# A layer's norms, recurrence and small network in one plan, its roots as GpSimd powers

## The reference, cut to what matters

```python
x = x + _mamba(_layernorm(x, ln1_g, ln1_b), in_proj_w, conv_w, ...)
h = _layernorm(x, ln2_g, ln2_b)
h = relu(einsum('btd,hd->bth', h, w1) + b1)      # 512 hidden
x = x + einsum('bth,dh->btd', h, w2) + b2
```

## Time and profile before

| | us |
|---|---|
| Median of three runs | 3910.06 (3905.43 to 3916.63) |
| The profiled execution | 3907.57, its span 3906.2 |
| Last layer, stages 1 and 2, to the first convolution | 2353.4 to 2413.1 |
| Stage 3 | 2413.1 to 2779.2 |
| Stage 4 | 2779.5 to 2875.5 |
| Stage 5 | 2876.0 to 3906.2 |

### The profile page before, as it was taken

The page is one execution under the profiler, slowest core; times in us unless marked ns, Lnnn a source line. Parts: engine busy times, 40 slices in busy tenths (PEclk is TensorE's granted clock), DMA queues, the critical chain, the costliest instruction groups (busy, mean ns, idle before and its releaser), DMA issues.

```text
span 3906.2 us, 43056 instructions
## 1 busy us (share of the span) xinstructions
PE 3027.4 (78%) x15912; PEld 1384.5 (35%) x16002; DVE 2560.6 (66%) x2915; ACT 2032.3 (52%) x3628; POOL 1557.2 (40%) x938
## 2 busy tenths in 40 slices
PE   4899989755678777777767798766778888888876
PEld 2233333412223222223224524211335555554544
DVE  4888724399987888888883243877446565565553
ACT  1566641344567676676662213676345556555544
POOL 2221101134566666766672011444234444344432
PEclk7899989766788888777878798888789998998998
DMA  3222100211111221121120002001000000000000
GB/s 87 46 43 41 26 2 0 79 38 26 36 37 32 48 45 37 37 50 40 27 47 11 1 0 77 22 22 27 6 10 20 20 11 20 10 20 20 10 16 26
DMA packets 79742, 114.48 MB, mean 29 GB/s; under 512 B 16270, under 2 KB 49422, under 8 KB 78106
## 3 DMA queue, kind: packets, MB, share of 16 engines
q1 hardware_dynamic: 68268, 103.06, 11.0%
q0 software_dynamic: 11264, 8.66, 1.6%
HBM read 37.70 MB, written 17.33 MB: 14 GB/s over the span
## 4 chain that ended last, share of the span: by engine, by line
PE 48%; DVE 22%; ACT 15%; issue 7%; POOL 3%; DMA 2%; SPq 1%; POOLq 0%; DVEq 0%; ACTq 0%
DVE layer_mamba_state L1348 8%; DVE psum L1336 4%; PE psum L1120 3%; PE psum L2468 3%; ACT layer_mamba_decay L1274 3%; PE psum L2499 3%; PE psum L1197 3%; PE psum L783 2%; PE psum L236 2%; PE psum L2162 2%; PE psum L248 2%; PE psum L242 2%; PE psum L913 2%; PE psum L2552 2%; ACT L1274 2%
## 5 line engine op out<-in xcount | busy, mean ns | idle before, releaser
L1377 POOL TENSOR_TENSOR layer_mamba_state<-layer_mamba_state,layer_mamba_c 128x1024 f32<-128x1024 f32 x320 | 781.2, 2450 | 593.2 <-DVE layer_mamba_state L1348 588.6
L1348 DVE TENSOR_TENSOR_SCAN layer_mamba_state<-layer_mamba_decay,psum 128x1024 f32<-128x1024 f32 x320 | 731.5, 2286 | 44.4 <-ACT layer_mamba_decay L1274 12.0
L1197 PE MATMUL psum<-layer_mamba_state,two_to_one 128*64 128x512 f32 x1280 | 440.1, 780 | 127.7 <-DVE layer_mamba_x L1365 82.2
L1274 ACT ACTIVATE layer_mamba_decay<-layer_mamba_delta_wide,layer_weights 128x511 f32<-128x511 f32 x640 | 415.8, 711 | 77.6 <-DMA layer_mamba_delta_wide<-layer_mamba_delta 42.3
L1336 DVE TENSOR_TENSOR psum<-psum,layer_mamba_u_wide 128x1024 f32<-128x1024 f32 x320 | 393.3, 1229 | 65.4 <-PE psum L1155 27.5
L724 DVE TENSOR_REDUCE layer_peak<-psum 128x2 f32<-128x1024 f32 x256 | 308.6, 1221 | 95.0 <-PE psum L695 90.2
L796 ACT ACTIVATE layer_exps<-psum 128x1024 f32<-128x1024 f32 x256 | 256.0, 1023 | 149.8 <-PE psum L763 149.7
L2865 POOL TENSOR_TENSOR layer_p<-layer_p,layer_stats 128x512 f32<-128x512 f32 x128 | 133.2, 1041 | 297.8 <-DVE layer_stats L2788 297.7
L2659 ACT ACTIVATE layer_p<-psum,layer_stats 128x128 f32<-128x128 f32 x512 | 181.5, 369 | 128.4 <-DVE layer_stats L2781 128.0
L2852 POOL TENSOR_TENSOR layer_qk<-layer_qk,layer_v_between 128x1024 f32<-128x1024 f32 x64 | 150.5, 2351 | 218.2 <-DVE layer_v_between L2752 216.4
L1155 PE MATMUL psum<-layer_mamba_bc,layer_mamba_pick 96*64 96x512 bf16 x768 | 165.0, 457 | 87.0 <-DVE psum L1336 63.3
(11 more groups left out here) (349 smaller groups left out, 6072.9 us busy)
## 6 DMA issues: line engine op xcount, KB each, us to landing
layer_mamba_delta_wide<-layer_mamba_delta SPq DMA_DIRECT2D x160, 128.0 KB, 2.4
layer_mamba_u_wide<-layer_mamba_work SPq DMA_DIRECT2D x160, 128.0 KB, 2.4
layer_v_between<-layer_v SPq DMA_DIRECT2D x16, 512.0 KB, 4.3
qk_dram<-layer_qk_parts SPq DMA_DIRECT2D x16, 384.0 KB, 2.9
layer_q_rows<-qk_dram SPq DMA_DIRECT2D x96, 64.0 KB
layer_k_rows<-qk_dram SPq DMA_DIRECT2D x96, 64.0 KB
layer_v_between<-layer_v SPq DMA_DIRECT2D x16, 384.0 KB, 5.6
layer_weights<-weights_dram SPq DMA_DIRECT2D x1, 4147.0 KB, 14.2
```

The lines of the kernel that those rows point to most:

```text
L1197: e = pe.matmul(c.psum[j * HALF:(j + 1) * HALF, self.sum_banks[h], :], c.two_to_one[:, :], self.state[i % len(self.state)][:, j, :], start ...
L1274: e = act.activation(decay[:, j, 1:SEQ], self.delta_wide[h][:, j, 1:SEQ], ACT.Exp, scale=rates[:, rate:rate + 1])
L1348: dve.tensor_tensor_scan(state, decay, self.fill.rearrange("p j t -> p (j t)"), 0.0, ALU.mult, ALU.add).then_inc(self.scanned, 1)
L1377: pool.tensor_tensor(state, state, self.both(self.c_wide[turn % self.C_BUFFERS][:, :]), ALU.mult).then_inc(self.multiplied, 1)
```

## The change

Stages 1 to 4 become one stage with one plan. `NormBeside` replaces `Norm` there, three times: "norm3" (x to xn, called O below), "norm1" (F) and "norm2" (S). Of each one sequence is in flight. Its root and reciprocal are one GpSimd power (add eps on ScalarE by Identity, then `pow` -0.5 on a 128x4 tile). The normed input has two buffers instead of eight, the hidden tile one instead of two. The small network's steps are planned behind S. z's silu moves next to x's. TensorE starts behind `conv_made`. The mask and tables on GpSimd are due at 50. In stage 5 the due times move: make 7.8 apart for 7.5, weigh 11.6 behind its score for 10.4, and the norm's, gates' and pass's. After the barrier each engine has one more drain.

```diff
-    start=40.0, pace=4.4, item=0.0, spread=-3.4, c_spread=-3.0, copy=-2.0, decay=-4.5, conv=((0.2, 0.8, 1.4, 2.0),), x=(2.7,), z=2.6, z_gate=3.2,
+    start=85.0, pace=4.4, item=0.0, spread=-3.4, c_spread=-3.0, copy=-2.0, decay=-4.5, conv=((0.2, 0.8, 1.4, 2.0),), x=(2.9,), z=2.6, z_gate=2.95,
...
-MAKE_PACE3, WINDOW_PACE3, TURN_AFTER3 = 7.5, 6.5, 8.0
+NORMS3 = (-10.9, -7.8, 3.6)
+STEPS3 = (0.0, 2.0, 3.2, 5.0, 6.8, 7.8, 10.0, 12.2, 13.2)
+HIDDEN_PACE3, TABLES3 = 1.2, 50.0
+MAKE_PACE3, WINDOW_PACE3, TURN_AFTER3, WEIGH_AFTER3 = 7.8, 6.5, 8.0, 11.6
 MAKE3 = [2.0 + MAKE_PACE3 * t for t in range(BLOCKS)]
 ROOT3 = MAKE3[-1] + 6.5
 SCALE3 = [ROOT3 + 2.6 + 2.1 * t for t in range(BLOCKS)]
 TURN3 = [SCALE3[0] + 2.4 + 2.5 * t for t in range(BLOCKS)]
 SCORE3 = [TURN3[1] + 3.0 + WINDOW_PACE3 * m for m in range(WINDOWS3)]
-OUT3 = SCORE3[-1] + TURN_AFTER3 + 4.6
-NORM3 = [OUT3 + 6.4 + t for t in (0.0, 1.3, 2.1, 2.8, 3.9, 5.6, 5.9, 8.0, 8.8)]
-GATE3 = NORM3[-1] + 1.0
+OUT3 = SCORE3[-1] + WEIGH_AFTER3 + 2.2
+NORM3 = [OUT3 + 6.4 + t for t in (0.0, 1.3, 2.4, 4.4, 5.4, 6.4, 7.6, 8.8, 9.8)]
+GATE3 = NORM3[-1] + 2.6
 MLP3 = GATE3 + 9.8
-PASS3 = MLP3 + 5.0
+PASS3 = MLP3 + 6.0
 UPDATE3 = PASS3 + 0.2
...
+        self.conv_made = c.sem(ctx, "conv_made")
+    def make_conv(self):
+        pool, hold, w = self.c.pool, self.c.pool_hold, self.w
         by_tap = lambda t: t.rearrange("p (k e) -> p k e", k=8)
-        hold.wait_ge(loaded, 16)
+        hold.wait_ge(self.loaded, 16)
         pool.tensor_tensor(by_tap(self.conv[""][:, :]), by_tap(w["conv_rows"]),
-                           w["w_x"].rearrange("p (o e) -> p o e", o=1).broadcast_to([P, 8, P]), ALU.mult)
+                           w["w_x"].rearrange("p (o e) -> p o e", o=1).broadcast_to([P, 8, P]), ALU.mult).then_inc(
+            self.conv_made, 1)
+    def tables(self, wf, ffn_loaded):
+        pool, hold, w = self.c.pool, self.c.pool_hold, self.w
+        yield TABLES3
         pool.tensor_copy(self.mask[:, :], w["masks"])
         hold.wait_ge(ffn_loaded, 16)
...
+class NormBeside:
+    def __init__(self, c, ctx, banks, name, src, out, times, gain=None, bias=None):
...
+        c.pool.memset(self.power[:, :], -0.5).then_inc(self.power_set, 1)
+        self.done = self.scaled if gain is None else self.biased
...
+    def pe(self, ready):
+        c, pe, hold = self.c, self.c.pe, self.c.pe_hold
+        hold.wait_ge(c.constants_made, c.constants)
+        for b in range(SEQS):
+            start = self.times(b)
+            yield start
+            at = self.banks.take((self.name, "mean", b), start, start + STEPS3[1] + 0.9)
+            if ready:
+                hold.wait_ge(ready, b + 1)
+            c.wait_bank(at)
+            pe.matmul(c.psum[:, at, :], c.mean_of[:, :], self.src(b), start=True, stop=True).then_inc(self.mean_made, 1)
+            c.bank_read[at] = self.mean_taken, b + 1
+            now = start + STEPS3[3]
+            yield now
+            at = self.banks.take((self.name, "var", b), now, start + STEPS3[4] + 0.4)
+            hold.wait_ge(self.squared, b + 1)
+            c.wait_bank(at)
+            for j in range(BLOCKS):
+                m = pe.matmul(c.psum[:, at, j:j + 1], self.square[:, j * P:(j + 1) * P], c.mean_of[:, 0:1], start=True,
+                              stop=True)
+            m.then_inc(self.var_made, 1)
+            c.bank_read[at] = self.var_kept, b + 1
+            now = start + STEPS3[6]
+            yield now
+            at = self.banks.take((self.name, "spread", b), now, start + STEPS3[7] + 0.9)
+            hold.wait_ge(self.inverse_made, b + 1)
+            c.wait_bank(at)
+            for j in range(BLOCKS):
+                m = pe.matmul(c.psum[:, at, j * P:(j + 1) * P], self.scale[:, 1, j:j + 1].broadcast_to([P, P]),
+                              c.ident[:, :], start=True, stop=True)
+            m.then_inc(self.spread_made, 1)
+            c.bank_read[at] = self.scaled, b + 1
+    def act(self, free):
+        c, act, hold = self.c, self.c.act, self.c.act_hold
+        for b in range(SEQS):
+            start = self.times(b)
+            yield start + STEPS3[2]
+            hold.wait_ge(self.mean_taken, b + 1)
+            act.activation(self.square, self.centred, ACT.Square).then_inc(self.squared, 1)
+            yield start + STEPS3[4]
+            hold.wait_ge(self.var_made, b + 1)
+            act.activation(self.scale[:, 0, :], self.bank("var", b)[:, 0:BLOCKS], ACT.Identity, bias=c.eps[:, :]).then_inc(
+                self.var_kept, 1)
+            if self.gain is not None:
+                yield start + STEPS3[8]
+                signal, value = free
+                hold.wait_ge(signal, value(b))
+                hold.wait_ge(self.scaled, b + 1)
+                act.activation(self.out(b), self.centred, ACT.Identity, bias=self.bias).then_inc(self.biased, 1)
+    def dve(self):
+        dve, hold = self.c.dve, self.c.dve_hold
+        for b in range(SEQS):
+            start = self.times(b)
+            yield start + STEPS3[1]
+            hold.wait_ge(self.mean_made, b + 1)
+            hold.wait_ge(self.done, b)
+            dve.tensor_tensor(self.centred, self.src(b), self.bank("mean", b), ALU.subtract).then_inc(self.mean_taken, 1)
+            yield start + STEPS3[7]
+            hold.wait_ge(self.spread_made, b + 1)
+            if self.gain is None:
+                dve.tensor_tensor(self.out(b), self.centred, self.bank("spread", b), ALU.mult).then_inc(self.scaled, 1)
+            else:
+                dve.scalar_tensor_tensor(self.centred, self.centred, self.gain, self.bank("spread", b), ALU.mult,
+                                         ALU.mult).then_inc(self.scaled, 1)
+    def pool(self):
+        pool, hold = self.c.pool, self.c.pool_hold
+        hold.wait_ge(self.power_set, 1)
+        for b in range(SEQS):
+            yield self.times(b) + STEPS3[5]
+            hold.wait_ge(self.var_kept, b + 1)
+            pool.tensor_tensor(self.scale[:, 1, :], self.scale[:, 0, :], self.power[:, :], ALU.pow).then_inc(
+                self.inverse_made, 1)
 class Attention3:
...
+    def __init__(self, c, ctx, x, xn, w, loaded, setup, out, tables):
+        self.c, self.x, self.xn, self.w, self.loaded, self.out = c, x, xn, w, loaded, out
+        self.normed = [c.buffer(ctx, f"normed{s}", [P, SEQ]) for s in range(2)]
+        self.inner = c.buffer(ctx, "mlp_normed", [P, SEQ])
+        self.hidden = c.buffer(ctx, "hidden", [P, HID_BLOCKS3, SEQ])
+        self.more = c.buffer(ctx, "more", [P, SEQ])
+        self.banks = Banks(5)
+        self.mamba = mamba = Mamba(c, ctx, w, loaded, setup.conv, 1, 8, SEQS, ("",), PLAN3, self.banks, 5, (7,))
+        self.opening = NormBeside(c, ctx, self.banks, "norm3", lambda b: x[:, b, :], lambda b: xn[:, b, :],
+                                  lambda b: PLAN3.front(b, NORMS3[0]))
+        self.first = NormBeside(c, ctx, self.banks, "norm1", lambda b: xn[:, b, :], lambda b: self.normed[b % 2][:, :],
+                                lambda b: PLAN3.front(b, NORMS3[1]), w["ln1_g"], w["ln1_b"])
+        self.second = NormBeside(c, ctx, self.banks, "norm2", lambda b: out[:, b, :], lambda b: self.inner[:, :],
+                                 lambda b: PLAN3.after(b, NORMS3[2]), w["ln2_g"], w["ln2_b"])
+        c.pe_hold.wait_ge(setup.conv_made, 1)
+        play(merged(mamba.pe(lambda u: self.normed[u % 2][:, :], lambda u: w["w_out"]), self.opening.pe(None),
+                    self.first.pe(self.opening.done), self.second.pe(self.residual_added), self.pe_mlps()))
+        play(merged(mamba.act(lambda u: out[:, u, :]), self.opening.act(None), self.first.act((mamba.z_made, lambda b: b - 1)),
+                    self.second.act((self.hidden_made, lambda b: HID_BLOCKS3 * b)), self.act_mlps()))
+        c.dve_hold.wait_ge(loaded, 16)
+        play(merged(mamba.dve(), self.opening.dve(), self.first.dve(), self.second.dve()))
+        play(merged(tables, mamba.pool(), self.opening.pool(), self.first.pool(), self.second.pool(), self.pool_residuals(),
+                    self.pool_mlps()))
         play(mamba.sp())
+    def mlp_time(self, b):
+        return PLAN3.after(b, NORMS3[2]) + STEPS3[-1] + 1.2
+    def pe_mlps(self):
+        c, pe, hold, w = self.c, self.c.pe, self.c.pe_hold, self.w
+        for b in range(SEQS):
+            start = self.mlp_time(b)
+            for f in range(HID_BLOCKS3):
+                now = start + HIDDEN_PACE3 * f
+                yield now
+                at = self.banks.take(("hidden", b, f), now, now + 2.0)
+                hold.wait_ge(self.second.done, b + 1)
+                c.wait_bank(at)
+                pe.matmul(c.psum[:, at, :], w["w1"][:, f * P:(f + 1) * P], self.inner[:, :], start=True,
+                          stop=True).then_inc(self.hidden_made, 1)
+                c.bank_read[at] = self.hidden_kept, HID_BLOCKS3 * b + f + 1
+            now = start + HIDDEN_PACE3 * HID_BLOCKS3 + 2.0
+            yield now
```

(57 more changed lines are left out.)

97 lines of the change are left out of this document (22 added, 75 removed).

## The result

The changed kernel takes 3854.26 us (median of 4 runs, 3852.63 to 3855.93) where the kernel before took 3911.99 beside it: a ratio of .985, interval .9834 to .9867. It is 57.7 us faster. The forecast was 3888 us, a gain of 22; the time lies in its range (3825 to 3935), but the gain is 36 us larger. The profiled execution of after has a span of 3851.5 us, 54.7 less than before's.

What follows compares the result with a forecast made beforehand. TensorE was taken to bound stage 4 and the last stage, VectorE the recurrence. Terms -10.4 + 62.6 - 73.9 + 0 = -21.7 took 3907.57 to 3885.9; with 2.5 for the median, 3888 us, range 3825 to 3935.

Steps and rivals of the forecast that it cites:

- (a): Start of the last layer to the first fill: 87.4 us before, 77 forecast, 10.4 us saved.
- (b): Recurrence, first fill to last scan: a chain through the engines' ordered lists, 53.8 us a sequence for 42.8, 62.6 us longer.
- rival B: Recurrence: the ring does not close and VectorE still sets the pace, 44.5 us a sequence, 3841 us in all; chance .18.
- the allowance of 1.5%: Recurrence: 6 us added because the same walk gave the old period as 42.2 us for 42.8.
- The table loads: ScalarE in the recurrence: two of six loads a sequence go, 2.6 us saved, all counted in the chain.
- The power: GpSimd's power in the norms: taken as .20 us, the lower bound, with 2.36 as the upper; no row shows it.
- (c): Last scan to the last stage: 107.0 us before, 33.1 forecast, 73.9 us saved, as seven of eight networks are done.
- (d): Last stage: only the order changes, 4.5 us of waits a pass gone and 4.8 added, taken as 0.
- Rival C: Last stage: new due times free more than they cost, 4 us a pass in some 12 passes, 3840 us; chance .12.
- Rivals D: Recurrence: a granted clock near .7 makes each period 10.1 us longer than forecast, 3938 us in all; chance .15.
- E: Norms in the recurrence: GpSimd's power costs 5 us, half of it on the ring, 3926 us in all; chance .05.
- F: Last stage loses 1.7 us a pass by its order, 20 us, so the kernel ends at 3908, no change; chance .08.

Runs made afterwards that it cites:

- a_early: Changed kernel with the waits for the loaded weights, and the work on them, put behind the first norms on each engine: 3835.42 us, ratio .9803.
- a_more: Changed kernel with the network's second product due 33.0 behind its first, just ahead of the next sequence's hidden products: 3823.45 us, ratio .9777.
- a_filler: Changed kernel with four idle products of 128x512 on TensorE just ahead of the hidden products, nothing moved: 3847.57 us, ratio .9835.
- a_tables: Changed kernel with x's and z's silu due apart again, as before, for two more table loads a sequence: 3855.31 us, ratio .9852.
- a_sqrt: Changed kernel with the three norms' root as ScalarE's Sqrt and VectorE's reciprocal again instead of GpSimd's power: 3849.24 us, ratio .9842.
- b_fill: Kernel before with four idle products a pass in its last stage, two ahead of the variance and two ahead of the gates: 3875.41 us, ratio .9904.
- Weigh only: Kernel before with only weigh, its copy and the out product due 1.2 later in the last stage: 3912.76 us, ratio .9999.
- make only: Kernel before with only make 7.8 apart for 7.5 in the last stage: 3890.83 us, ratio .9937.
- norm only: Kernel before with only the later due times of the norm's steps, gates and pass in the last stage: 3875.06 us, ratio .9899.

## Why the prediction was right and wrong

- **(a), to the first fill: right.** 11.1 saved for 10.4. (22.0 + 54.6 is 76.6, so the working gives 10.8; it was rounded to 77.) The convolution's weights came 20.5 us behind their issue, 1.4 earlier than before's, and the 54.6 us behind them were 55.7. That TensorE must wait for the weights first was taken as given; a_early shows that only the order made it so.
- **(b), the recurrence: right in kind, too long by 21.6.** The period is a ring of orders and not VectorE's work (rival B: 44.5), which the walk of its pieces and a_more's 45.6 show. Of the 21.6, 6 were the allowance of 1.5%, which only made it worse; 7.4 lie in the three whole periods (51.3 for 53.8), 8.2 in the five others. The 2.5 of a period are three terms: VectorE's piece was 1.4 too long (16.2 for 17.6), the piece from convolution to split .4 (25.7 for 26.1), and the clock's surcharge .7: it was laid on all of TensorE's 23.8 us at .88, 3.2, where it fell on one piece behind one wait, 2.5, as a_filler shows. An average clock does not say where the low clock lies.
- **The table loads: wrong as a term.** The 2.6 us that the chain counted for two loads were .9 by a_tables. The Trainium skill ("ScalarE: Activation LUTs", What ACT_TABLE_LOAD costs) would have it a load and 1380 ns more; no run shows that: with five loads more a sequence the recurrence kept its length, and on the ring one load added 1.4, where the load itself is 1.28.
- **The power: the value was too low, and it did not matter.** It takes 1.01 us for the .20 taken, within the bounds of .20 and 2.36. Its place off the ring is what saved the sum: the recurrence is as long without it (369.3).

```profile
L2375 POOL TENSOR_TENSOR layer_norm_scale<-layer_norm_scale,layer_norm_power x24: 1000/1010/1051, 2386.4 to 2825.9; 128x4 f32<-128x4 f32 x24
```

  The Trainium skill ("GPSIMD Engine Reference", 4.1 Engine selection) puts GpSimd at about twice VectorE's time for two inputs; here the power took 1.01 against .18 for the reciprocal it replaces, more than five times. The two are not the same operation, so this doesn't measure the rule; its direction spoke against the edit, and a_sqrt, 5 us faster by median with overlapping intervals, is on its side.
- **(c), from the last scan on: 6.3 too short.** The prediction let the last sums follow at once (10.2 from the last scan to the end of the residual, as before); S's mean starts 16.2 behind the last scan, and that is nearly all of the 6.3. In after VectorE waits 11.40 for them, since the seventh network stands ahead of them in TensorE's order:

```profile
2802.88 3.78 PE L2431 MATMUL psum<-layer_mlp_normed,layer_weights 128*128 128x512 f32 x4 [1.30 <-ACT layer_mlp_normed L2351]
2806.59 1.98 PE L1197 MATMUL psum<-layer_mamba_state,two_to_one 128*64 128x512 f32 x4
...
2811.57 3.70 PE L2440 MATMUL psum<-layer_hidden,layer_weights 128*128 128x512 f32 x8
2815.21 1.08 PE L1197 MATMUL psum<-layer_mamba_state,two_to_one 128*64 128x512 f32 x4
```

  With the seventh network's second product moved behind them (a_more) the whole part is 35.9 us for 39.4.

- **(d), the last stage: wrong, and this is the miss of the mechanism.** The count of waits was right: 4.5 gone and 4.8 added a pass were forecast, and the trace has 68.1 to 72.4 in nine passes, +.5 a pass. The step that failed is the sentence that at .92 "the clock has little to give", by which the last stage was put at 0. The stage gained 23.0 us, and in nine passes the low clock fell from 41 to 15 us. A share of .08 of 470 us is 38 us in nine passes, over half as much as all waits together, and filling two waits takes most of it away (b_fill). Rival C came near the time (3840) by a wrong mechanism: it had fewer waits. Rival B (3841) was as near, by a period of 44.5 for the 51.3 measured.
- **The chances.** Rivals D, E and F did not come. That the clock could be a gain in the last stage was not among the cases.

Left open: which pattern of waits lowers the clock. "Weigh only" has one wait of 3.7 and one of 1.9 in place of two short ones and loses as much as before; "make only" has the norm's two waits down to .6 and 1.0, others of up to 1.7, and loses nearly as much; "norm only" has one of 2.4 and many of up to 1.6 and loses little. Nor was it tried why make at 7.8 and weigh at 11.6 give back 17 us beside the norm's moves (992.7 to 1007.1 with the same stage ahead).

## What to carry to other kernels

Split TensorE's time into work at full clock, waits, and low clock behind waits, before an order is judged. In the last stage the norm's two waits, 3.7 us a pass, cost another 3.4 us of low clock behind them (41 less 10 in nine passes); in other orders waits as long cost little. When every engine runs a fixed list, follow the ring piece by piece: what takes work off a piece, or puts it into the ring's own wait, shortens the period, and what only lightens an engine (most table loads here) need not. And look at a stage's first waits: one that is there for a later step holds all that stands behind it.

## What the runs showed of the hardware

Idle products made a kernel faster: 36 of them in nine passes, 31 us of work, took the granted clock there from .92 to .98 and the nine passes from 549.4 to 520.5 us; the whole last stage, with 64 of them, went from 1030 to 986 us. In the recurrence four of them ahead of the hidden products (1.88 for 3.78 behind them) took 2.3 us off a period of 51.3. A GpSimd power on 128x4 takes 1.00 to 1.05 us, as much as a cast of 128x1024 to bf16 there (1.04).
